# Router scores as silu(x)/x instead of 1/(1+exp(-x)), and the routing pieces one step later

## The reference, cut to what matters

```
h = relu(xn @ nm_w1 + nm_b1);  m = h @ nm_w2 + nm_b2
q, k, v = m @ q_w + q_b, m @ k_w + k_b, m @ v_w + v_b
attention over a window of 32 tokens to either side, softmax, weights @ v

scores = sigmoid(xn @ gate_w.T)                # 16 experts
inds   = top_k(scores + expert_bias, 8)
w      = scores[inds] / sum(scores[inds]) * 2.826
y      = sum_e w_e * down_e(silu(gate_e(xn)) * up_e(xn)) + the shared expert
```

## Time and profile before

| | |
|---|---|
| median of 3 runs | 683.89 us (683.76 to 684.17) |
| time of the profiled execution | 684.41 us |
| its span in the trace | 682.6 us |
| PE busy | 673.7 us, 99% |
| DVE busy | 615.5 us, 90% |
| ACT busy | 448.1 us, 66% |
| POOL busy | 431.3 us, 63% |
| granted TensorE clock | full in every slice |

### The profile page before, as it was taken

How to read it: one execution, slowest core, us unless ns; L and a number is a source line. 1 busy time by engine, 2 the same in 40 slices (tenths; PEclk the granted TensorE clock), 3 DMA queues, 4 the chain that set the end, 5 groups by cost and what they waited for, 6 DMA issues and landing times.

```text
span 682.6 us, 10378 instructions
## 1 busy us (share of the span) xinstructions
PE 673.7 (99%) x3080; PEld 543.5 (80%) x3080; DVE 615.5 (90%) x1687; ACT 448.1 (66%) x918; POOL 431.3 (63%) x386
## 2 busy tenths in 40 slices
PE   8999999999999999999999999999999999999997
PEld 6877788788888878788887888888888787888875
DVE  6999999999999999999999999999899999898875
ACT  5875666657676575766766676576766757576573
POOL 4785665666657656676566657656676566656553
PEclk9999999999999999999999999999999999999999
DMA  8607155261633717155271642717245171532600
GB/s 266 238 2 290 51 174 199 85 243 57 231 130 102 270 34 279 61 164 210 61 265 48 219 153 97 270 38 264 79 145 227 42 279 39 198 144 62 233 1 16
DMA packets 38040, 101.80 MB, mean 149 GB/s; under 512 B 8672, under 2 KB 18144, under 8 KB 29920
## 3 DMA queue, kind: packets, MB, share of 16 engines
q1 hardware_dynamic: 37984, 101.14, 41.7%
HBM read 92.42 MB, written 8.70 MB: 148 GB/s over the span
## 4 chain that ended last, share of the span: by engine, by line
PE 87%; DVE 5%; DMA 3%; ACT 2%; issue 1%; SPq 1%; DVEq 0%; ACTq 0%
PE ps_u L511 25%; PE ps_y L521 25%; PE ps_g L501 25%; PE bank L432 3%; DVE ps_u L1193 1%; PE bank L481 1%; PE ps_y L491 1%; PE bank L472 1%; PE bank L465 1%; PE bank L443 1%; DMA exp_raw<-wexp 1%; DVE h_lo L1199 1%; DMA h_dram<-exp_raw 1%; PE bank L454 1%; PE bank L483 1%
## 5 line engine op out<-in xcount | busy, mean ns | idle before, releaser
L1325 POOL TENSOR_TENSOR silu_c<-silu,comb_b 128x512 f32<-128x512 f32 x252 | 326.9, 1300 | 229.2 <-ACT silu L766 229.2
L774 ACT ACTIVATE h_hi<-ps_u 128x512 fp32r<-128x512 f32 x272 | 163.2, 600 | 217.6 <-DVE ps_u L1193 217.5
L1199 DVE TENSOR_TENSOR h_lo<-ps_u,h_hi 128x512 fp32r<-128x512 f32 x272 | 185.5, 682 | 26.8 <-ACT h_hi L774 23.7
L1193 DVE TENSOR_TENSOR ps_u<-silu_c,ps_u 128x512 f32<-128x512 f32 x256 | 176.7, 690 | 16.9 <-PE ps_u L511 11.7
L766 ACT ACTIVATE silu<-ps_g 128x512 f32<-128x512 f32 x272 | 161.8, 595 | 0.2
L511 PE MATMUL ps_u<-xn_hi,exp_w_hi 128*128 128x512 f32 x272 | 112.4, 413 | 1.3 <-DVE h_lo L1199 1.2
L521 PE MATMUL ps_y<-h_hi,exp_w_hi 128*128 128x512 f32 x272 | 109.0, 401 | 0.9 <-DVE h_lo L1199 0.6
L501 PE MATMUL ps_g<-xn_hi,exp_w_hi 128*128 128x512 f32 x272 | 108.2, 398 | 1.3 <-ACT silu L766 1.3
L521 PE MATMUL ps_y<-h_lo,exp_w_hi 128*128 128x512 f32 x272 | 107.4, 395 | 0.0
L521 PE MATMUL ps_y<-h_hi,exp_w_lo 128*128 128x512 f32 x272 | 107.3, 395 | 0.0
L511 PE MATMUL ps_u<-xn_hi,exp_w_lo 128*128 128x512 f32 x272 | 107.3, 395 | 0.0
(11 more groups left out here) (160 smaller groups left out, 960.6 us busy)
## 6 DMA issues: line engine op xcount, KB each, us to landing
comb_b<-c_dram SPq DMA_DIRECT2D x63, 1024.0 KB, 7.2
mom_b<-st_dram SPq DMA_DIRECT2D x13, 512.0 KB, 3.8
xres<-x_t SPq DMA_DIRECT2D x16, 256.0 KB, 2.6
out_t<-xres SPq DMA_DIRECT2D x16, 256.0 KB, 2.0
xin<-x SPq DMA_DIRECT2D x15, 256.0 KB, 3.0
h_dram<-exp_raw SPq DMA_DIRECT2D x60, 64.0 KB
exp_raw<-h_dram SPq DMA_DIRECT2D x15, 256.0 KB, 3.1
xn<-x_t SPq DMA_DIRECT2D x13, 256.0 KB, 3.3
```

Source lines behind the costliest of these rows:

```text
L774: A(h_t[hbuf(par, s)][0][:], ps_u[(par + s) % 2][:], ACT.Copy).then_inc(s_h_hi, 1)
L1193: V.tensor_tensor(ps_u[i][:], src[:], ps_u[i][:], ALU.mult).then_inc(s_h, 1)
L1199: V.tensor_tensor(t[1][:], ps_u[(par + s) % 2][:], t[0][:].bitcast(F32), ALU.subtract)\
L1325: G.tensor_tensor(silu_c[i][:], silu[i][:], comb_b[:, s1 - 1, :], ALU.mult).then_inc(s_silu_c, 1)
```

## The change

The router's sigmoid is made another way: instead of exp(-x), plus 1 and a reciprocal, it is silu(x) times the reciprocal of x. An x too near to zero is first moved to a small number. That takes three new small operations on POOL, between DVE's reduce (which now writes `gate_1`) and `gate_s`. DVE takes the reciprocal of `gate_s` in one slot (`route_inverse`) and multiplies it by ACT's silu in a later one (`route_scores`). In later groups `gate_sig` runs on ACT in slot 7 instead of 5, `route_inverse` on DVE in slot 7, `route_scores` with `route_max` in slot 9, `route_match` in 10, `route_sum` in 11 and `route_weights` in 12, behind `hid_blocks`. `prob_lo` moves by one slot too. In the first group `off_zero` is in POOL's slot 8 and `route_inverse` in DVE's slot 9, before `h_lo`. On SP, `store_hid` now comes before `store_comb`, and `load_hid` right after the first `spread`.

In the prologue ACT runs a Silu on one column first; side products use `bank[2]` instead of `ps_u[1]`; the second up projection comes ahead of the tiles of combine weights; and the casts `expw_hi(3)` and `(4)` come after the first silu.

```
+            def off_zero(g):
+                pool.wait_ge(S["gate_1"], g + 1)
+                G.tensor_tensor(near0[:], gate_1[:], gate_1[:], ALU.mult).then_inc(S["near0"], 1)
+                pool.wait_ge(S["near0"], g + 1)
+                G.tensor_scalar(near0[:], near0[:], TINY * TINY, 2.0 * TINY, ALU.is_lt, ALU.mult).then_inc(S["moved0"], 1)
+                pool.wait_ge(S["moved0"], g + 1)
...
+                G.tensor_tensor(gate_s[:], near0[:], gate_1[:], ALU.add).then_inc(S["gate_s"], 1)

-            def gate_exp(g):
+            def gate_sig(g):
                 act.wait_ge(S["gate_s"], g + 1)
...
-                A(flat(gate_e), flat(gate_s), ACT.Exp, scale=-1.0).then_inc(S["gate_e"], 1)
+                A(flat(gate_e), flat(gate_s), ACT.Silu).then_inc(S["gate_e"], 1)

+            def route_inverse(g):
+                dve.wait_ge(S["gate_s"], g + 1)
+                V.reciprocal(inv_gate[:], gate_s[:]).then_inc(S["inv_gate"], 1)

             def route_scores(g):
...
-                V.tensor_scalar(gate_1[:], gate_e[:], 1.0, None, ALU.add).then_inc(S["gate_1"], 1)
-                dve.wait_ge(S["gate_1"], g + 1)
-                V.reciprocal(score[:], gate_1[:]).then_inc(S["score"], 1)
+                dve.wait_ge(S["inv_gate"], g + 1)
+                V.tensor_tensor(score[:], gate_e[:], inv_gate[:], ALU.mult).then_inc(S["score"], 1)

 DVE att(g, par, s)
-                if s == 7 and more and not first(g):
-                    route_scores(g + 1)
+                if s == when(g, 7, 9) and more:
+                    route_inverse(g + 1)
                 if s == when(g, 8, 11):
                     normalise_probs(g, 1)
-                if s == when(g, 8, 10) and more:
+                if s == when(g, 9, 10) and more:
+                    route_scores(g + 1)
                     route_max(g + 1)
-                if s == when(g, 9, 12):
+                if s == when(g, 10, 12):
                     prob_lo(g, 0)
-                if s == when(g, 9, 10) and more:
+                if s == when(g, 10, 11) and more:
                     route_match(g + 1)
-                if s == when(g, 10, 13):
+                if s == when(g, 11, 13):
                     prob_lo(g, 1)
-                if s == when(g, 10, 11) and more:
+                if s == when(g, 11, 12) and more:
                     route_sum(g + 1)
-                if s == when(g, 11, 12) and more:
-                    route_weights(g + 1, 1 - par)
...
                 if s == 12 and more:
                     hid_blocks(g + 1)
+                    route_weights(g + 1, 1 - par)
```

More of the change, by code:

```diff
@@ L31 @@
 TAKEN = -3e38
+TINY = 1e-15
 RUNS = 8
@@ L229, in layer @@
         names = """bn aggr var_eps rstd mean centred0 centred1 xn xn_tp xn_hi xn_lo gate_mm gate_h gate_s gate_e
-            hid_b gate_1 score select top8 rest weight wsum winv comb comb_t
+            hid_b gate_1 near0 moved0 inv_gate score select top8 rest weight wsum winv comb comb_t
             hid_mm hid hid_hi hid_lo q_mm q_hi q_lo hid_tp hn_hi hn_lo key_term
@@ L672, in slot @@
                     gate_proj(*after(g, par, s))
+                if first(g) and s == 1:
+                    up_proj(g, par, s)
                 att_early(g, par, s)
@@ L676, in slot @@
                 att_late(g, par, s)
-                up_proj(g, par, s)
+                if not first(g) or s != 1:
+                    up_proj(g, par, s)
                 if first(g) and s == 3:
@@ L776, in prologue @@
             def prologue():
+                act.wait_ge(s_spin, 1)
+                A(warm[:], spin_in[:, 0:1].bitcast(F32), ACT.Silu)
                 act.wait_ge(s_watt_in, 16)
@@ L787, in prologue @@
                 expw_hi(2)
-                gate_exp(0)
-                expw_hi(3)
-                expw_hi(4)
+                gate_sig(0)
             def score_weights():
@@ L834, in att @@
                 if s == when(g, 5, 8):
-                    if more:
-                        gate_exp(g + 1)
                     prob_exp(g, 0)
+                if s == when(g, 7, 9) and more:
+                    gate_sig(g + 1)
                 if s == when(g, 7, 10):
@@ L854, in slot @@
                     act.wait_ge(s_side_mm, 1)
-                    A(chain[:, 1, :], ps_u[1][:, M_B:M_B + P], ACT.Copy).then_inc(s_side, 1)
+                    A(chain[:, 1, :], bank[2][:, M_B:M_B + P], ACT.Copy).then_inc(s_side, 1)
                 else:
@@ L1052, in prologue @@
                 gate_sum(0)
+                route_inverse(0)
                 route_scores(0)
@@ L1216, in slot @@
                     moments(1, 1)
-                if first(g) and s == 9:
-                    route_scores(1)
             def finish():
@@ L1279, in prologue @@
                 pool.wait_ge(S["xn"], 1)
-                for s in range(0, 3):
+                for s in range(0, 2):
                     expw_lo(s)
+                off_zero(0)
+                expw_lo(2)
                 pool.wait_ge(S["comb"], 1)
@@ L1337, in slot @@
                         centre(g + 2, 1)
+                if s == when(g, 5, 8) and not last(g):
+                    off_zero(g + 1)
                 if s == when(g, 2, 5):
```

35 lines of the change are left out of this document (24 added, 11 removed).

## The result

The changed kernel took 691.48 us, the median of five runs (691.10 to 692.16), and the kernel before 683.76 (683.56 to 684.17) beside it: 1.0115 times as long, 95% interval 1.0101 to 1.0129. The forecast was 691.8 us and slower. The profiled execution took 692.16, with a span of 690.3; the prediction had put these at 692.3 and 690.5.

What follows compares the result with a forecast made beforehand. PE bounds the kernel, busy throughout the later groups, with DVE next at 92%. Prologue 1.06, first group 2.9 and later groups 3.9 sum to 7.9 us, forecasting 691.8 us; its own range 689 to 694, overall 685.8 to 695.

Steps and rivals of the forecast that it cites:

- The later groups: Slot 9, groups 1 to 13: score's product waits for POOL's `silu_c`, delaying PE 0.30 us a group, 3.9 us together.
- SP's order: On SP, storing hidden blocks ahead of `store_comb` makes the first `spread` land just in time; counted as nothing.
- if the product isn't locked: Later groups, bound: product not held by POOL's `silu_c`, two small late starts of PE vanish, -0.14 us a group.
- Rival A: Later groups, slot 9: the product isn't locked or slips in ahead of `silu_c`; 685.9 us; chance 0.13.
- Rival B: Later groups: `select` is locked too, by the next `silu_c`, 1.5 us a group more; 711 us; chance 0.06.
- Rival D: Slots 5 to 9: ACT bounds more than seen; removing `gate_exp` gains about 0.3 us a group; chance 0.04.
- `off_zero` was free: Later groups: POOL's three new operations fall into its idle 4.28 us and cost nothing.
- The three small operations: Prologue, on POOL: reduce's end to `gate_s` takes 1.4 us, bounds 0.95 and 2.1 us.
- The prologue: DVE's path sets PE's start; `select` and all behind it come 1.06 us later, bounds +0.6 and +1.7.
- I count nothing for it: Prologue: the up projection moved ahead of the combine tiles fills PE's wait of about 0.7 us; counted as nothing.
- The first group: POOL's queue makes `gate_s` late, then DVE's reciprocal, `h_lo` and PE; +2.9 us, bounds 2.0 and 3.6.
- rival C: The first `spread` lands late, POOL, DVE and PE wait in 15 groups; 1 us late gives 704; chance 0.07.

Runs made afterwards that it cites:

- experiment 5: Changed kernel with the product making `score` replaced by a one-input reduce, leaving out the factor 1/x; 687.33 us, ratio 1.0046.
- experiment 6: Changed kernel with both the `score` product and `select` made one-input reduces, leaving out 1/x and the bias; 684.56 us, ratio 1.0007.
- experiment 9: Kernel before with `route_max` in slot 7 instead of 8 in the later groups; 682.15 us, ratio 0.9967.
- experiment 1: Changed kernel with PE's `hid_proj` waiting for `gate_1` instead of `gate_s`; 691.66 us, ratio 1.0114.
- experiment 3: Changed kernel with the second up projection back behind the tiles of combine weights; 691.43 us, ratio 1.0109.
- experiment 12: Changed kernel with the prologue's placement edits (side products, waits, second up projection) undone together; 691.43 us, ratio 1.0108.
- experiment 4: Changed kernel with `off_zero(1)` at the head of POOL's slot 8 in the first group, ahead of `silu_c`; 692.29 us, ratio 1.0123.
- experiment 8: Kernel before with only SP's new order, hidden blocks stored first and loaded back right after the first `spread`; 683.12 us, ratio 0.9986.
- experiment 2: Changed kernel with five spinning matmuls ahead of the first `hid_proj`; 692.09 us, ratio 1.0118.
- experiment 11: Changed kernel with `hid_proj` waiting for `gate_1`, `off_zero(1)` ahead in POOL's first-group slot 8, and `pow` in slot 9; 689.19 us, ratio 1.0075.

## Why the prediction was right

**The later groups: right, by mechanism and size.** 0.30 us a group was forecast for groups 1 to 13, and nothing for group 14. In groups 2 to 13 it was 0.29, in group 14 0.09, together 3.6 us, as forecast for them. Group 1 is told below, under SP's order. The product is held until POOL's `silu_c` ends (0.92 us, forecast about 0.9), the up projection behind it pays, and with the meeting taken away (experiments 5 and 6) the period falls by 0.25 and 0.43. That is more than the 0.30 forecast, down to 41.02, below the kernel before. The reason was in the prediction as the -0.14 of the bound "if the product isn't locked": experiment 9 gets the same 41.02 in the kernel before by emptying slot 8 alone. Rival A, then, had its gain of a group right, and its condition (a start 0.45 us earlier) didn't come. Rival B (`select` held by the next `silu_c`, 1.5 us a group) didn't come; where the product was spared, in experiment 5, it was the same `silu_c` that held `select`, for 0.43 us. Rival D (ACT bounds these slots) didn't come either. `off_zero` was free, as its place among POOL's idle time promised: 1.23 us in the earlier trace rows's gap.

**The three small operations: right.** 0.29, 0.45 and 0.32 us with 0.09 between them, from the reduce's end to `gate_s` 1.40 us; 1.4 was forecast by a line through larger operations. The premise that POOL is free by then held by luck: in experiment 1 it wasn't, and the same stretch took 2.18 us.

**The prologue: the forecast held for the chain, not for the profiled execution.** +1.06 us was forecast, +2.02 measured. Of the chain's step, +1.00 is there. What was mis-sized stood at nothing: the clock, which had no term, and the sentence "I count nothing for it", for the up projection moved ahead of the tiles. With matmuls at 0.43 us the tiles are late, and `silu_c` waits 1.20 us, 0.70 for the order and 0.50 for the clock (experiment 3). At the full clock (experiment 12, where it is moved back) the start is +1.09. Even that sum is right by luck in part: the reduce came 0.26 us earlier there, and 0.41 us were lost at a place that I had not looked at, `hid_lo` (1.10 us in place of 0.69), another operation with two inputs, which now meets an `exp_w_lo`. In fourteen later groups of the kernel before it takes 1.16 to 1.18 us too, so its rows were there to be read.

**The first group: right in size, wrong in what binds.** 2.9 us was forecast and 2.77 measured, and each wait is where it was said to be: the reciprocal's, 2.11 us of PE, `score` and `select` locked, slot 12. But the working added up PE's waits, from `gate_s` on, as if the first caused the loss. Experiment 4 takes 1.7 us from it and gains nothing. The limit is POOL's queue, to whose `silu_c` DVE's routing is tied: with the product freed from it, 0.95 of the 2.77 us are gone (experiment 5). `off_zero` adds 1.2 us to that queue, which is a likely cause of more of it, but not one that a run shows. So the right size is luck in part.

**SP's order: wrong, and the largest miss of a term.** "I count nothing" was said of it, with rival C as the danger. The median landing of the transfers into `comb_b` did grow (8.3 us instead of 7.2), and no one waited for them: every `silu_c` that waited started within 0.15 us of the end of ACT's silu, as in the kernel before. C is refuted here. Overlooked was what the order gives, for I looked only at who becomes late: in the group behind the first, the load of the hidden blocks comes earlier and ACT's wait of 1.93 us goes. That group takes 42.75 us instead of 43.39, -0.64 where +0.30 had been forecast, and experiment 8 shows -0.92 for it by itself.

**The sum.** At the markers: 2.02 + 2.77 - 0.64 + 12 x 0.29 + 0.09 = 7.7, against 7.9 forecast. The two misses, +0.96 and -0.94, cancelled: that is luck. A reader who takes the total as proof of its terms would be taken in.

Two things stay open. Without the 0.96 the changed kernel's trace would be one of 691.2 us, and its other runs took 691.1 to 691.8, so that fits. But the trace of the kernel before took 684.41, 0.65 above its median, and so of the 7.7 us between the medians the markers without the 0.96 explain 6.8. The prologue's dates differ by up to 0.7 us from trace to trace (the reduce ends between 10.99 and 11.67 in the kernels here), and I can't resolve more. And what lowers the clock more often in the changed kernel. In experiments 2, 4, 6 and 11 it fell between 10.8 and 11.4, ahead of any empty stretch at `hid_proj`, and in experiment 11 there was none (PE worked on). Neither that stretch nor the side products' new wait (12) decides it alone, and the kernels differ in the first group's empty 2.1 us as well, behind which it fell in three traces.

## What to carry to other kernels

When DVE work is moved, look for each operation with two inputs in SBUF (and, by the rows of experiment 5, for `TENSOR_SCALAR` too) which of POOL's operations it then meets: here 0.23 us became 0.92, and it is the meeting that must be moved, since freeing one operation hands the wait to the next. A wait of PE that ends on a late date is a symptom; ask whether the date behind it is set by another engine's whole queue before an earlier start is credited (experiment 4: 1.7 us taken from one wait, none won). And take a change apart even where it loses: one of its parts, SP's order, and a relief that another had brought, slot 8 without `route_max`, made the kernel before 0.46% faster.

## What the runs showed of the hardware that I had not expected

- An operation's end under the lock is that of POOL's operation and most of its own work: with 64 columns it ended 0.08 or 0.09 us after POOL's (the ones shown above, of 0.66 to 1.28 us), and with 512 columns, `hid_lo`, 0.55 us after (21.52 against 20.97), of its own 0.69.
- One input in SBUF doesn't free every DVE operation: a `TENSOR_SCALAR` of 64 columns took 0.73 us in place of 0.19 and ended 0.06 after POOL's.
- TensorE's clock fell to the lower level for 3 to 7 us after 1.3 us without work in one execution, not after 1.5 or 2.1 us in others, ahead of the empty stretch in four, and within one kernel in some runs and not in others. The Trainium skill (TensorE: Matmul & The Clock Gate, Part 1: The HAM clock gate) says of the first matmuls of a kernel that how many run at the lower clock differs from run to run; the runs agree, and show it of later stretches too. In 9 of 10 profiled executions of the changed kernels the mean clock was 0.997 or lower, in 10 of 38 others. So a lower clock seen in one profile must be looked for in the other runs' mean clock before it is made part of an explanation.
- Half the clock costs what is left of PE's slack. Some 3.4 us of it in the first group of experiment 12, and as much in experiment 2, moved the marker by 0.02 us, since PE would have waited for DVE anyway. In experiment 6 the same place was at 0.57, and its marker came 40.33 us behind the first down projection instead of experiment 5's 39.39: there it seems to have eaten what the freed operations had won (no trace of that kernel at the full clock is kept).
